# Token selection: logits with tokens on the output's partitions, brought to batches by identity products, and a Sinkhorn of sums by halves

## What is computed

```python
def _L0_ffn_ref(x, gate_query, log_temp, w1, b1, w2, b2):
    gate_logits = jnp.einsum('bnd,ed->ben', x, gate_query)
    affinity_logits = gate_logits / jnp.exp(log_temp)
    t = affinity_logits                       # _sinkhorn
    for _ in range(6):
        t = t - logsumexp(t, axis=-2, keepdims=True)   # over the experts
        t = t - logsumexp(t, axis=-1, keepdims=True)   # over the tokens
    affinity = jnp.exp(t)
    gates, idx = jax.lax.top_k(affinity, 32)  # CAP
    ...
x = x + jnp.tanh(g_ffn[0]) * _L0_ffn_ref(_layernorm(x, axis=-1), ...)
```

## Time and profile before

| | |
|---|---|
| median of 3 runs | 2228.38 us (2228.18 to 2230.93) |
| the profiled execution | 2227.19 us, span 2225.3 us |
| TensorE busy | 93% of the span |
| VectorE busy | 78% |
| ScalarE busy | 72% |
| GpSimd busy | 29% |

### The profile page before, as it was taken

One profiled execution on the slowest core, in us unless ns is written; L12 is line 12 of the kernel. 1 busy time (PEld: TensorE's weight loads), 2 busy tenths in 40 slices (PEclk: granted clock), 3 DMA queues, 4 the chain that ended last, 5 costly groups with the idle time before them and its releaser, 6 DMA issues. The chain is left out here.

```text
span 2225.3 us, 74451 instructions
## 1 busy us (share of the span) xinstructions
PE 2061.3 (93%) x26251; PEld 1382.5 (62%) x26251; DVE 1740.4 (78%) x3815; ACT 1595.8 (72%) x2792; POOL 653.7 (29%) x890
## 2 busy tenths in 40 slices
PE   6999999676699999999999999699999999999798
PEld 4666666433266666666666667566666666666576
DVE  4888887569688888888888887688888888888544
ACT  4777777455588888888888888566666667777433
POOL 3666666411000000000000000044555444444464
PEclk8999999778699999999999999899999999999799
DMA  7111101238000000000000000111111110000133
GB/s 175 28 33 32 33 27 32 52 136 314 18 13 12 10 12 11 13 9 11 9 13 10 13 6 2 50 53 62 61 53 61 62 44 6 5 5 4 43 103 104
DMA packets 105115, 96.76 MB, mean 43 GB/s; under 512 B 35920, under 2 KB 90048, under 8 KB 104640
## 3 DMA queue, kind: packets, MB, share of 16 engines
q1 hardware_dynamic: 104464, 95.51, 14.1%
q10 hardware_dynamic: 560, 0.08, 0.0%
HBM read 56.00 MB, written 31.10 MB: 39 GB/s over the span
## 5 line engine op out<-in xcount | busy, mean ns | idle before, releaser
L1604 DVE TENSOR_TENSOR h<-g,h 128x1024 f16<-128x1024 f32 x256 | 313.5, 1225 | 160.5 <-ACT h L1549 159.7
L231 PEld LDWEIGHTS psE<-ew,h 128*128 128x128 f16 x6144 | 360.3, 98 | 54.1 <-issue 29.0
L231 PE MATMUL psE<-ew,h 128*128 (+1 forms) x6144 | 380.6, 219 | 7.8 <-DVE eo L1615 7.2
L231 PE MATMUL psH<-xg,ew 128*128 (+1 forms) x1536 | 355.3, 381 | 2.3 <-issue 1.6
L1544 ACT ACTIVATE g<-psH,eb1T 128x512 f32<-128x512 f32 x512 | 322.8, 679 | 35.3 <-PE psH L231 24.1
L570 PE MATMUL psV<-Bw,cT 96*64 96x512 f16 x2064 | 287.8, 386 | 3.0 <-DVE vB L749 3.0
L723 POOL TENSOR_TENSOR E<-E,rden 128x512 f32<-128x512 f32 x192 | 200.3, 1043 | 291.7 <-DVE rden L758 291.7
L1549 ACT ACTIVATE h<-g 128x1024 f16<-128x1024 f32 x256 | 270.6, 1057 | 16.2
L714 POOL TENSOR_TENSOR Ph<-E,Ph 128x512 f16<-128x512 f32 x192 | 222.4, 1158 | 179.5 <-ACT Ph L674 179.5
L655 ACT ACTIVATE vB<-psV 128x512 f16<-128x512 f32 x344 | 202.6, 589 | 79.8 <-PE psV L570 79.8
L1675 POOL MEMSET rbias<- 64x384 f32 x1 | 0.4, 412 | 879.8 <-POOLq L132 879.8
(11 more groups left out here) (253 smaller groups left out, 3106.0 us busy)
## 6 DMA issues: line engine op xcount, KB each, us to landing
keys_ahead<-ust SPq DMA_DIRECT2D x40, 512.0 KB, 4.7
u<-keys_ahead SPq DMA_DIRECT2D x40, 512.0 KB, 3.4
rawe<-in_L_ffn_w_dram SPq DMA_DIRECT2D x32, 256.0 KB, 2.8
wb<-rw SPq DMA_DIRECT2D x64, 128.0 KB, 2.0
rows<-places SPq DMA_DIRECT2D x110, 64.0 KB, 2.6
out_dram<-x SPq DMA_DIRECT2D x7, 512.0 KB, 3.2
context_T<-cT SPq DMA_DIRECT2D x64, 48.0 KB, 1.5
cT<-context_T SPq DMA_DIRECT2D x64, 48.0 KB, 1.8
```

The lines of the kernel that those rows point to most:

```text
L231: last = e.matmul(to, a, b, start=start and n == 0, stop=stop and n == 2, **flags)
L1604: e.tensor_tensor(h[:, 1 - par, 1, 2 * q:2 * q + 2, :], g32[:, 2 * q:2 * q + 2, :], h[:, 1 - par, 0, 2 * q:2 * q + 2, :], ALU.subtract)\
```

## The change

The logits are made with the tokens' block as the stationary side and the gate query, now of 16 columns, moving. The output has a token on each partition and, for each tile, 16 experts beside each other, so that eight steps fill one bank of `psL`. VectorE scales a bank by the token's factor, which now lies on the same partition as the token, in one operation (`scaled`), and TensorE brings it to batches by products with the identity (`by_batch`): for each expert, a product from the 64 tokens of either batch of a tile. Batch 2t + side is then on partition 64 side + t, in `psZ`. No logits and no factors go through DRAM. The 17 operations of the normalisation stand behind the copies of steps 0 to 5, three by three.

In the Sinkhorn block the sums and maxima over the experts are made by halving: 8 rows of 64 onto 8, 4 onto 4, 2 onto 2, 1 onto 1, all contiguous. The first round subtracts the maximum over the experts, takes the exponential for the sums over the experts, subtracts the maximum over tokens and takes a second exponential for the sums over tokens; no logarithm is taken. Since partitions hold batches in another order, the stores of shares and places are made for either side apart, and the identity's columns in the slots' products and in `run_experts` are read in that order.

```diff
-            rs = sb(c, "rs", [P, N], F32)
-            lg_dram = nc.dram_tensor("gate_logits", [B, NE, N], F32).ap()
-            rs_dram = nc.dram_tensor("token_scale", [NT, P], F32).ap()
+            rs = sb(c, "rs", [P, NT], F32)
...
-                        e.wait_ge(s["rsT"], 1)
-                        e.dma_start(rs_dram, rsT[:]).then_inc(s["rs_out"], 16)
-                        e.wait_ge(s["rs_out"], 16)
-                        e.dma_start(rs[:], rs_dram.rearrange("t (b n) -> (t b) n", n=N)).then_inc(s["rs"], 16)
-                        for j in range(STEPS):
-                            e.wait_ge(s["l"], j + 1)
-                            for k in range(LT):
-                                t = LT * j + k
-                                e.dma_start(lg_dram[2 * t:2 * t + 2].rearrange("b e n -> e b n"),
-                                            L[32 * k:32 * k + NE, j % 2, :].rearrange("e (b n) -> e b n", n=N))\
-                                 .then_inc(s[f"lg_out{j % 2}"], 16)
-                        for par in range(2):
-                            e.wait_ge(s[f"lg_out{par}"], 16 * LT * STEPS // 2)
-                        e.dma_start(lg[:], lg_dram).then_inc(s["lg"], 16)
...
                             par = j % 2
                             e.wait_ge(s["xT"], j + 1)
-                            if j >= 2:
-                                e.wait_ge(s["l"], j - 1)
-                            for n, (gl, xl) in enumerate(((0, 0), (0, 1), (1, 0))):
-                                for k in range(LT):
-                                    last = e.matmul(psL[32 * k:32 * k + 32, par, 0:P], gq[:, gl, :], xT[:, par, xl, k, :],
-                                                    start=n == 0, stop=n == 2)
+                            for k in range(LT):
+                                t = LT * j + k
+                                for n, (gl, xl) in enumerate(((0, 0), (0, 1), (1, 0))):
+                                    last = e.matmul(psL[:, t // HT, NE * (t % HT):NE * (t % HT) + NE],
+                                                    xT[:, par, xl, k, :], gq[:, gl, :], start=t % HT == n == 0,
+                                                    stop=t % HT == HT - 1 and n == 2, skip_group_check=True)
                             last.then_inc(s["L"], 1)
 
+                        def by_batch(hf):
+                            e.wait_ge(s["l"], hf + 1)
+                            for k in range(NE):
+                                for side in range(2):
+                                    rows = slice(64 * side, 64 * side + 64)
+                                    to = slice(64 * side + HT * hf, 64 * side + HT * hf + HT)
+                                    e.matmul(psZ[to, k, :], L[rows, hf, :, k], ident32[rows, rows], start=True, stop=True)
...
-                            if j == 2:
-                                e.wait_ge(s["v"], 17)
-                                e.wait_ge(s["gq_lo"], 1)
-                                e.transpose(psG[0:NT, P:2 * P], rstd[:], ident32[:]).then_inc(s["rT"], 1)
                             if j >= 1:
                                 logits(j - 1)
+                            if j == STEPS // 2 + 2:
+                                by_batch(0)
...
+                        by_batch(1)
...
-                        def out(j):
-                            e.wait_ge(s["L"], j + 1)
-                            if j >= 2:
-                                e.wait_ge(s[f"lg_out{j % 2}"], 16 * LT * (j // 2))
-                            e.activation(L[:, j % 2], psL[:, j % 2, 0:P], ACT.Copy).then_inc(s["l"], 1)
...
-                        queue_norm(e, s, lnt, 0, ALL)
+                        e.tensor_tensor(gq[:, 1], psG, gq[:, 0], ALU.subtract).then_inc(s["gq_lo"], 1)
+
+                        def scaled(hf):
+                            tiles = slice(HT * hf, HT * hf + HT)
+                            e.wait_ge(s["L"], STEPS // 2 * (hf + 1))
+                            e.wait_ge(s["rs_t"], 1)
+                            e.tensor_tensor(L[:, hf], psL[:, hf].rearrange("p (t e) -> p t e", e=NE),
+                                            rs[:, tiles].unsqueeze(2).broadcast_to([P, HT, NE]), ALU.mult)\
+                             .then_inc(s["l"], 1)
+
                         for j in range(STEPS):
                             e.wait_ge(s["X"], j + 1)
                             if j >= 2:
                                 e.wait_ge(s["L"], j - 1)
                             e.tensor_copy(xT[:, j % 2], psX[:, j % 2]).then_inc(s["xT"], 1)
+                            if j < NORM_STAGES:
+                                queue_norm(e, s, lnt, 0, ALL, j)
+                            if j == NORM_STAGES:
+                                e.wait_ge(s["v"], 17)
+                                e.wait_ge(s["rt"], 1)
+                                e.tensor_scalar(rs[:], rstd[:], temp[:, 1:2], None, ALU.mult).then_inc(s["rs_t"], 1)
+                            if j == STEPS // 2 + 1:
+                                scaled(0)
                             if j == 8:
                                 e.wait_ge(s["fold_hi"], 1)
                                 e.tensor_tensor(folded[2], folded[0], folded[1], ALU.subtract)
+                        scaled(1)
...
-                        e.wait_ge(s["lg"], 16)
-                        e.wait_ge(s["rs_t"], 1)
-                        e.tensor_tensor(lg[:], lg[:], rs[:].unsqueeze(1).broadcast_to([P, NE, N]), ALU.mult)
...
+                    by_side = [places.rearrange("(t q) c -> q t c", q=2),
+                               shares.rearrange("h e (t q) n -> q t h e n", q=2)]
+                    for side in range(2):
+                        for hl in range(2):
+                            e.dma_start(by_side[1][side][:, hl], share16[64 * side:64 * side + 64, hl])\
+                             .then_inc(s["shares"], 16)
                     e.wait_ge(s["idx16"], 1)
-                    e.dma_start(places, idx16[:]).then_inc(s["places"], 16)
-                    e.wait_ge(s["places"], 16)
-                    e.wait_ge(s["shares"], 32)
+                    for side in range(2):
+                        e.dma_start(by_side[0][side], idx16[64 * side:64 * side + 64, :]).then_inc(s["places"], 16)
...
+                    def exps(turn):
+                        for hf in range(2):
+                            e.wait_ge(s[f"d{turn}"], hf + 1)
+                            e.activation(z[:, halves[hf]], (lg, z)[turn][:, halves[hf]], ACT.Exp, bias=zero_col[:])\
+                             .then_inc(s[f"e{turn}"], 1)
+
+                    keep(0, 2)
+                    exps(0)
+                    keep(2, 5)
+                    exps(1)
+                    keep(5, 8 * GROUPS)
...
+                    def tree_over_e(frm, op, to):
+                        e.tensor_tensor(tree, frm[:, 0:8], frm[:, 8:16], op).then_inc(s["it"], 1)
+                        e.wait_ge(s["it"], next(done))
+                        e.tensor_tensor(tree[:, 0:4], tree[:, 0:4], tree[:, 4:8], op).then_inc(s["it"], 1)
+                        e.wait_ge(s["it"], next(done))
+                        e.tensor_tensor(tree[:, 0:2], tree[:, 0:2], tree[:, 2:4], op).then_inc(s["it"], 1)
+                        e.wait_ge(s["it"], next(done))
+                        e.tensor_tensor(to, tree[:, 0], tree[:, 1], op).then_inc(s["it"], 1)
+                        e.wait_ge(s["it"], next(done))
+
+                    def rows_to_one():
+                        e.tensor_reduce(rmax[:, 1], lg[:], AX.X, ALU.add).then_inc(s["it"], 1)
+                        e.wait_ge(s["it"], next(done))
+                        e.reciprocal(rmax[:, 1], rmax[:, 1]).then_inc(s["it"], 1)
+                        e.wait_ge(s["it"], next(done))
+                        e.tensor_tensor(lg[:, halves[0]], lg[:, halves[0]], over_n(rmax[:, 1], 0), ALU.mult)
+                        e.tensor_tensor(lg[:, halves[1]], lg[:, halves[1]], over_n(rmax[:, 1], 1), ALU.mult).then_inc(s["it"], 1)
+                        e.wait_ge(s["it"], next(done))
+
+                    e.tensor_copy(lg[:, halves[0]], psZ[:, halves[0]]).then_inc(s["it"], 1)
+                    e.wait_ge(s["it"], next(done))
+                    e.tensor_tensor(tree, lg[:, halves[0]], psZ[:, halves[1]], ALU.max).then_inc(s["it"], 1)
+                    e.wait_ge(s["it"], next(done))
+                    e.tensor_tensor(tree[:, 0:4], tree[:, 0:4], tree[:, 4:8], ALU.max).then_inc(s["it"], 1)
+                    e.wait_ge(s["it"], next(done))
+                    e.tensor_tensor(tree[:, 0:2], tree[:, 0:2], tree[:, 2:4], ALU.max).then_inc(s["it"], 1)
+                    e.wait_ge(s["it"], next(done))
+                    e.tensor_tensor(total[:], tree[:, 0], tree[:, 1], ALU.max).then_inc(s["it"], 1)
+                    e.wait_ge(s["it"], next(done))
+                    for hf in range(2):
```

(37 more changed lines are left out.)

107 lines of the change are left out of this document (32 added, 75 removed).

## The result

| | before | the change |
|---|---|---|
| median | 2228.28 us (2227.56 to 2230.93) | 2206.39 us (2203.54 to 2207.03) |
| ratio | | 0.9897, 95% interval 0.988 to 0.9914 |
| the profiled execution | 2227.19, span 2225.3 | 2206.2, span 2204.3 |
| TensorE, VectorE, ScalarE, GpSimd busy | 93, 78, 72, 29% | 93, 79, 72, 30% |

The change is faster by 21.9 us; I had forecast 16.2 (2211.5, with a range of 2202 to 2223). Medians are of four executions each. The stretches by time of the changed kernel, cut at the same events as the earlier trace rows: start of the logits block, first product of the keys, first round's end, first pick. Behind the stretch and its length stand the busy us of TensorE, its weight loads, VectorE, ScalarE and GpSimd (with instructions), the granted clock, and DMA.

A forecast was written before the change was run, and what follows sets the result against it. The prediction saw token selection as the hollow stretch, its logits block bound by a chain across engines plus a trip through memory. Logits -11.1, Sinkhorn -5.8, stores +0.7 summed to -16.2 us: 2211.5, range 2202 to 2223.

The forecast's parts named there:

- the products' price: Logits block, TensorE: twelve products with token-block weights and 16 moving columns taken at 0.7 us, between 0.44 and 1.4.
- first identity group: Logits block: 32 f32 identity products of 64 columns, added behind step 10, taken at 2.8 us.
- 15 plain steps: Logits block: 15 steps of 1.7 us each, between the chain's 1.5 and TensorE's 1.9.
- normalisation beside GpSimd: Steps 0 to 5 of the logits block: VectorE's small operations sometimes wait on GpSimd, 2.0 us in all (0 to 8.4).
- fold transposes and products: Logits block, TensorE: second-layer weight fold stays, eight transposes and eight products, taken at 1.6 and 1.2 us.
- tail from there: Logits block's end: last copy 0.8, last products 0.9, scaling 0.8, identity products 2.8, hand-over 0.8 us.
- that rival: Logits block: TensorE rises to 2.4 GHz for most of it, step 1.3 us, total 2202; chance 0.13.
- the rival's 8.4: Steps 0 to 5: VectorE's queue bounds, each stage waiting out two GpSimd subtractions; 8.4 us for 2.0, total 2218; chance 0.10.
- The Sinkhorn block: Forecast 5.8 us less (3 to 8): first round 12.8 for 15.1, later rounds 6.41 for 7.1, five giving 3.5.
- The rival of rounds no cheaper: Sinkhorn block: eleven operations, nearly each behind a wait, save nothing of the 5.8 us; total 2217; chance 0.05.
- the slower one: Logits block: 192 short products cannot hide weight loads, some 0.2 us each, step 3.6; +13.2, total 2240; chance 0.04.
- The end: End of the selection: twice as many store issues on SyncE for shares and places, 0.7 us later (0 to 2.5).

## Why the prediction was right, and where its terms were off

The sign, the mechanism and the order of the terms hold: the trip through memory is gone, the steps set the logits block, both parts add. The gain was 5.7 larger than forecast, and the time still in the range. By the parts the forecast was less near than the total says: the selection won 23.4 for 16.2, and the attention and what follows, in which nothing changed, gave back 2.4 of that in this trace. That the time came out within the range and not at its fast edge is in part luck. The sum of the logits block was too high in nearly every term. Of the surplus of 8.0, 3.0 is the products' price, about 2.2 the clock in the steps, 2.8 the fold and the first identity group, 1.4 the tail and the first copy; against them stand 1.5 by the reading of the normalisation used here. Step by step, in the order of the prediction's sum (times from the start of the logits block; measured in the trace of the change):

| step of the prediction | forecast | measured |
|---|---|---|
| first copy | 3.3 | 3.0 |
| 15 plain steps | 25.5 | 20.3 (the remainder: 1.35 each) |
| normalisation beside GpSimd | 2.0 | 3.5 by the run without it (0.7 at like clock) |
| fold transposes and products | 2.8 | 1.3 |
| first identity group | 2.8 | 1.5 |
| last copy begins | 36.4 | 29.6 |
| tail from there | 6.1 | 5.0 |
| the block | 42.5 | 34.6 |

The fold and the identity group are read from the copies around them: 2.22, 2.11 and 2.77 us from one copy to the next, less a plain step's 1.5, 1.5 and 1.29. The plain steps' 20.3 is what is left, so it hangs on the normalisation's 3.5, the upper end of what the runs give; with 0.7 a plain step would be 1.54. Steps seen by themselves stand 1.46 and 1.49 apart at the low clock (second to fourth copy) and 1.29 in the last ones at the high clock, not the 1.7 that I had named as a sign.

- **The products' price was mis-sized.** I said 0.7 for twelve, between 0.44 and 1.4; they took 0.49 to 0.51 at the low clock and 0.45 at the high one, and the next transposes begin 0.37 behind their start (435.56 to 435.93). With 0.81 from the transposes' start to theirs (428.70 to 429.51), TensorE's step is 1.2 at the low clock and not 1.9, below the chain's 1.5, and the mean of 1.7 between the two had no ground: it should have been 1.5. That is about 3.0 of the 8.0 that the block gained over the forecast. The transposes load the same form of weights (128x128 f16) and follow each other every 0.12, these products every 0.041: the load cannot be what sets the transposes' 0.12, so that row was far too high a bound for a product of 16 columns. The Trainium skill (TensorE: Matmul & The Clock Gate, Weight-path perf modes — Fast Weight Load (FWL) and DoubleRow) describes a faster load for 128 weights of a type other than FP32, and has about 40 ns a product for FP8 products of few columns that keep it. The trace's 41 ns is of that size; that this path is the reason no run here shows. The section on LDWEIGHTS that the prediction weighed gives 107 ns for the load, and the trace disagrees: twelve loads and products took 0.49 together.
- **The clock** is the other part of the steps: from about 437 on it was 2.4 GHz, the chain's step became 1.3 as that rival said, and the identity products cost 2.05 and 2.69. About 2.2 of the plain steps' surplus would be that (1.5 to 1.35), by the reading of the normalisation above. The outcome in this trace is the forecast's mechanism for nine or ten steps and the rival's for the rest; taking them as exclusive was the fault. In size the block's 19.1 lies nearer to that rival's 21 than to the forecast's 11.1, but not by the clock alone: the other three traces of the same block had more or other stretches at 2.4 GHz and took 33.62 to 34.73, so the course of the clock moved it by about 1 us.
- **The normalisation's collisions** cost 0.7 to 3.5, so the 2.0 taken is neither confirmed nor refuted, and the rival's 8.4 is. Seven of the 17 operations were stretched, by 4.8 us in all. The Trainium skill's rule (SBUF — State Buffer, SBUF: two separate sides) says that the one that comes second waits out the whole instruction of the other; the rows agree, the operation from 429.44 ended at 430.53, the subtraction before it at about 430.5. The rival's condition, that each stage waits out two subtractions, did not come about: GpSimd rests while it waits for ScalarE (1.80 before 429.30), and ten of the 17 operations were not stretched.
- **The fold and the first identity group** were taken as if fully on the chain. A part lies in the waits that the chain leaves to TensorE anyway; together they cost 2.8 for 5.6 in this trace. For the group's share the run that moved it to the end has 1.37 from that copy to the next where it was 2.77.
- **The Sinkhorn block**: first round 12.84 for 12.8. Rounds 6.55 for 6.41: the tree is exact, the reciprocal of 64 columns took 0.59 with its wait for the 0.50 taken, and each multiplication 1.33 for 1.31. Five rounds gave 2.8 for 3.5. The rival of rounds no cheaper is refuted by the run of the Sinkhorn alone: 5.5 us shorter with it.
- **A slip in a rival**: the slower one's +13.2 on the 2227.7 that the forecast starts from gives 2241, not 2240; nothing hangs on it.
- **The end**: 0.67 for 0.7, and the key products stayed hidden: picks took 36.5 before and after.

Not tested: why the first and the second attention take 4 to 5 us more in some executions. The totals of all edits of the change lie nearly within that, so the order of the faster versions by total is not settled. By the logits block, and by single traces, only the longer one with the normalisation ahead and the shorter ones without it and with f32 transposes and one group at the end stand clear of the unedited block's own 33.62 to 34.73. Nor does a run part the 20 us won in the logits block into the trip through memory and the shorter step; the traces show both gone, the waits for stores and the wait of 8.66 for the load.

## What to carry to other kernels

Price an unseen matmul shape by the pitch of a run of them, and ask which operand sets the pitch in the row you borrow: here the rows' 120 ns came from 128 moving columns, and products with the same load under 16 columns took a third of it. A chain over four engines gives the step by its own sum; average it with another engine's load only if that load is really larger. Small operations of VectorE that are stretched beside GpSimd cost only what the chain does not hide: 4.8 us of stretching were 0.7 to 3.5 on the block, and the row ahead of the loop cost 2.0 to 3.2 more. Work that stands between steps of such a chain belongs behind the last one, where it can run in one group. And take several traces of an unedited kernel before reading a microsecond in an edited one: here the clock took another course in each.

## What the runs showed of the hardware

- Products with 128x128 f16 weights and 16 moving columns follow each other every 41 ns at 1.2 GHz and 38 ns (0.45 for twelve) at 2.4 GHz: the clock hardly matters for them, while eight transposes go from 1.03 to 0.62.
- f32 identity products from 64 rows onto 32 output partitions: 64 records written to two quarters of the output took 3.60 to 3.63 at 1.2 GHz and 2.05 at 2.4 GHz, and 128 records written to four quarters in turn 3.57 to 3.65 at 1.2 GHz.
- The granted clock in the logits block took another course in each of the four traces of the unedited block (mean 0.70, 0.71, 0.75, 0.71), which lasted 33.62 to 34.73; in three of the four versions with f32 transposes it was back at 1.2 GHz for the identity products at the end. What decides it stays open.
- At 1.2 GHz the first four copies stand 2.13, 1.46 and 1.49 us apart both with 12 and with 24 of these products a step.
